# A product-key expert stage on one core: one-hots one step later, index search beside the greatest values, experts' values in six slots

## The reference, cut to what matters

```
xn = batchnorm(x1) * gamma + beta
q = xn @ w_q.T                                  # 2 sides x 8 heads x 128
sim = einsum('pbnhd,hkpd->pbnhk', q, keys)      # 2 sides x 8 heads x 32 keys
s, i = top_k(sim, 8)                            # per side
all_scores = sx[:, None] + sy[None, :]          # 64 sums per token and head
scores, pk = top_k(all_scores, 8)
idx = (ix * 32 + iy)[pk]                        # 8 of 1024 experts
o = gelu(x1 . key_in[idx]) * softmax(scores)
out = layernorm(x1 + sum over head, k of o * key_out[idx])
```

## Time and profile before

| what | value |
|---|---|
| runs of the kernel before | 503.2, 506.0 and 501.16 us; median 503.2 |
| the profiled execution | 506.19 us, with a span of 504.1 us |
| granted clock of TensorE, mean | 0.786 of full speed |
| busy: TensorE, VectorE, ScalarE, GpSimd | 366.8, 431.7, 243.5, 232.1 us |
| scatter, 8192 products of 64x16 | 94.0 us busy |
| experts_out, 1024 products | 90.2 us busy |
| experts_in, 512 products | 68.3 us busy |
| index search, 512 times two instructions | 82.7 and 37.4 us |
| hotx, 32 instructions | 74.9 us |
| weighing on GpSimd, 60 pieces | 77.7 us |

### The profile page before, as it was taken

How to read it: one execution, slowest core, us unless ns; L and a number is a source line. 1 busy time by engine, 2 the same in 40 slices (tenths; PEclk the granted TensorE clock), 3 DMA queues, 4 the chain that set the end, 5 groups by cost and what they waited for, 6 DMA issues and landing times.

```text
span 504.1 us, 24229 instructions
## 1 busy us (share of the span) xinstructions
PE 366.8 (73%) x10097; PEld 268.3 (53%) x10097; DVE 431.7 (86%) x2755; ACT 243.5 (48%) x398; POOL 232.1 (46%) x311
## 2 busy tenths in 40 slices
PE   5979855166647778786888689768787678878755
PEld 3445543034443557465748474646477347746655
DVE  1557986999999689989999999899999997995923
ACT  2897564355324433574365337443754472445222
POOL 1023350542449344646556474647382925282610
PEclk9979956678656877889797678877987796579769
DMA  8900000000000000000000000000000000000001
GB/s 241 180 1 1 1 1 0 1 1 5 3 5 2 3 4 3 5 3 25 6 1 4 25 5 1 6 25 3 3 6 25 3 3 4 25 3 4 23 5 44
DMA packets 7661, 8.95 MB, mean 18 GB/s; under 512 B 896, under 2 KB 6912, under 8 KB 7424
## 3 DMA queue, kind: packets, MB, share of 16 engines
q1 hardware_dynamic: 6976, 7.34, 5.5%
q10 hardware_dynamic: 576, 0.07, 0.1%
HBM read 5.31 MB, written 2.10 MB: 15 GB/s over the span
## 4 chain that ended last, share of the span: by engine, by line
PE 47%; DVE 17%; issue 14%; POOL 5%; ACT 4%; ACTq 0%; DVEq 0%; POOLq 0%
PE psum L895 17%; PE psum L871 13%; PE psum L882 9%; PE psum L851 6%; DVE idx L623 3%; DVE vals L615 3%; DVE picked L648 2%; DVE arena L679 2%; POOL code L259 2%; POOL arena L286 2%; DVE arena L683 1%; DVE arena L682 1%; DVE arena L676 1%; ACT L434 1%; POOL ixf L254 1%
## 5 line engine op out<-in xcount | busy, mean ns | idle before, releaser
L871 PE MATMUL psum<-arena 64*64 64x16 f16 x8192 | 94.0, 180 | 77.5 <-issue 67.1
L871 PEld LDWEIGHTS psum<-arena 64*64 64x64 f16 x8192 | 86.2, 117 | 94.5 <-issue 85.5
L895 PE MATMUL psum<-ko,arena 64*128 64x128 f32 x1024 | 90.2, 353 | 2.0 <-issue 2.0
L895 PEld LDWEIGHTS psum<-ko,arena 64*128 64x128 f32 x1024 | 86.7, 264 | 2.9 <-issue 2.5
L623 DVE FIND_INDEX8 idx<-vals,sims 128x8 uint32<-128x32 f32 x512 | 82.7, 186 | 0.0
L286 POOL TENSOR_TENSOR arena<-arena 128x512 f32<-128x512 f32 x60 | 77.7, 1328 | 4.3 <-ACT arena L426 4.3
L882 PE MATMUL psum<-x1T,trn 128*64 128x256 f32 x512 | 68.3, 423 | 12.6 <-ACT arena L434 12.6
L679 DVE TENSOR_TENSOR arena<-iota,listsT 128x4096 f16<-128x4096 f16 x32 | 74.9, 2339 | 0.0
L426 ACT ACTIVATE arena<-psum 128x1024 f32<-128x1024 f32 x32 | 32.6, 1018 | 72.5 <-PE psum L871 72.5
L882 PEld LDWEIGHTS psum<-x1T,trn 128*64 128x64 f32 x512 | 36.6, 152 | 51.1 <-ACT arena L434 24.3
L239 POOL TENSOR_TENSOR cand<-vals 128x128 f32<-128x128 f32 x16 | 9.4, 588 | 118.0 <-DVE vals L615 118.0
(11 more groups left out here) (117 smaller groups left out, 563.7 us busy)
## 6 DMA issues: line engine op xcount, KB each, us to landing
x<-in_L_attn_x_dram SPq DMA_DIRECT2D x8, 256.0 KB, 4.8
out_dram<-nat SPq DMA_DIRECT2D x7, 256.0 KB, 2.1
ko<-in_L_ffn_key_out_dram SPq DMA_DIRECT2D x2, 512.0 KB, 9.7
nat<-in_L_ffn_key_in_dram SPq DMA_DIRECT2D x2, 256.0 KB, 9.7
nat<-in_L_ffn_keys_dram SPq DMA_DIRECT2D x2, 128.0 KB, 5.6
out_dram<-nat SPq DMA_DIRECT2D x2, 128.0 KB, 1.7
nat<-in_L_attn_W_delta_dram SPq DMA_DIRECT2D x1, 64.0 KB, 2.8
nat<-in_L_attn_W_in_dram SPq DMA_DIRECT2D x1, 64.0 KB, 2.8
```

What stands on the lines that cost most here:

```text
L871: end = pe.matmul(psum[64 * e:64 * e + 64, at:at + NJ], hotx[rows, g, :, e], hotw[rows, part, g, :, e], start=(part == 0), stop=(part == 1))
L895: end = pe.matmul(y2[:, e, m % 2] if m < NS - 1 else y_last[:, e], gl[rows, m % 4, j, :], ko[rows, j, :], start=(j == 0), stop=(j == NJ - 1))
```

## The change

It does these things:

- One-hots, lists, halves and scatter of a step are done one step later than before: VectorE's step m now holds hots_of(m-2), and the loops run to NS + 2. On TensorE the scatter isn't split any more.
- VectorE does indices(m) and top_sums(m) straight after greatest(m), and pack to weights of m-1 after them.
- `weigh` works by halves of the tokens, two pieces each: the second half of step m-4 before the candidate sums, the first of m-3 after them.
- experts_in and gelus run in steps 0, 1, 3, 5 ... 13 in place of 1, 3 ... 15, and `gl` has six slots.
- The two products of hoty with the weight halves become one instruction; listsT is laid out by halves of the tokens for it.
- The scatter halves (14, 1) and (15, 1) go to banks 0 and 1 in place of 2 and 3.

The diff, cut to its core:

```diff
+    GL = 6
+    GELU_STEP = (0,) + tuple(range(1, NS - 2, 2))
...
+        def p_base(m, hf):
+            return 0 if m * 2 + hf in (2 * NS - 3, 2 * NS - 1) else b_p
...
-            def weigh(m):
-                wait(pool, "p_evac", m * 2 + 2)
+            def weigh(m, hf):
+                wait(pool, "p_evac", m * 2 + hf + 1)
                 wait(pool, "gelu_done", (m // 2 + 1) * JR)
...
-            for m in range(NS + 1):
+            for m in range(NS + 2):
+                if m >= 2:
+                    halves(m - 2)
+                if m >= 4:
+                    weigh(m - 4, 1)
                 if m < NS:
                     candidate_sums(m)
-                if m >= 1:
-                    halves(m - 1)
                 if m >= 3:
-                    weigh(m - 3)
+                    weigh(m - 3, 0)
                 if m < NS:
                     candidate_codes(m)
                     over_eighth(m)
...
             def gelus(q):
-                wait(act, "y2_mm", q * 2 - 2)
+                wait(act, "y2_mm", q * 2 - 4)
                 for r in range(JR):
                     if r == 2:
-                        signs(2 * q + 1)
+                        signs(GELU_STEP[q])
...
+            for m in range(NS + 2):
+                if m >= 3:
+                    p_out(m - 3, 0)
                 if m >= 2:
-                    p_out(m - 2, 0)
+                    lists_out(m - 2)
                 if m < NS:
                     exps(m)
...
                 if m + 1 < NS:
                     sims_out(m + 1)
                 if m + 2 < NS:
                     normed(m + 2)
+                if 1 <= m <= NS:
+                    high_copied(m - 1)
+                if m >= 3:
+                    p_out(m - 3, 1)
+                if m < NS:
+                    low_halves(m)
+                if 1 <= m <= NS:
+                    convert(m - 1)
+                if m in GELU_STEP:
+                    gelus(GELU_STEP.index(m))
...
             def indices(m):
+                wait(dve, "code_done", m)
...
             def top_sums(m):
+                wait(dve, "dt_done", m)
...
-                dve.tensor_tensor(hotw[:, 0, at], hoty[:, at], spread(2, NJ), ALU.mult)
-                dve.tensor_tensor(hotw[:, 1, at], hoty[:, at], spread(3, NJ), ALU.mult).then_inc(s["hot_done"], 1)
+                both = listsT[:, hf, 2:4, :].rearrange("p w (g s) -> p (w g) s", s=2).unsqueeze(2)
+                dve.tensor_tensor(hotw[:, :, at].rearrange("p w g j s -> p w (g j s)"),
+                                  hoty[:, at].rearrange("p g j s -> p (g j s)").unsqueeze(1).to_broadcast(
+                                      [P, 2, 32 * NJ * 2]),
+                                  both.to_broadcast([P, 64, NJ, 2]), ALU.mult).then_inc(s["hot_done"], 1)
...
-            for m in range(NS + 1):
+            for m in range(NS + 2):
                 if m < NS:
                     greatest(m)
-                if m >= 1:
+                    indices(m)
+                    top_sums(m)
+                if 1 <= m <= NS:
                     pack(m - 1)
                     pick(m - 1)
                     weights_and_codes(m - 1)
-                if m < NS:
-                    indices(m)
-                    top_sums(m)
-                if m >= 1:
-                    hots_of(m - 1, 0)
-                    if m >= 5 and m % 2:
+                if m >= 2:
+                    hots_of(m - 2, 0)
+                    if 5 <= m < NS and m % 2:
                         residual(m // 2 - 2)
-                    if m >= 6 and m % 2 == 0:
+                    if 6 <= m <= NS and m % 2 == 0:
                         scales(m // 2 - 3)
-                    hots_of(m - 1, 1)
+                    hots_of(m - 2, 1)
...
+            for m in range(NS + 2):
                 if m >= 2:
-                    scatter(m - 2, 1, 0, 12)
-                if 1 <= m < NS:
-                    lists_turned(m - 1)
-                if m >= 2:
-                    scatter(m - 2, 1, 12, 32)
+                    lists_turned(m - 2)
                 if m + 1 < NS:
                     scores(m + 1)
...
+                if m >= 3:
+                    scatter(m - 3, 1)
+                if m >= 4:
+                    wait(pe, "lists_evac", m - 1)
+                    experts_out(m - 4)
+                if m in GELU_STEP:
+                    experts_in(GELU_STEP.index(m))
+                if m >= 2:
+                    scatter(m - 2, 0)
```

## The result

| kernel | runs | median, us | lowest to highest |
|---|---|---|---|
| before | 4 | 504.5 | 501.2 to 506.0 |
| after | 4 | 510.4 | 510.2 to 512.3 |

The measured ratio is 1.017, 95% interval 1.012 to 1.023 (the two medians alone give 1.012): slower, where the forecast was 496 us. That the change is slower is clear of noise; whether it is slower by 2% is not. The profiled execution has a span of 508.4 us; its granted clock is 0.768 (0.786 before).

What follows compares the result with a forecast made beforehand. TensorE bounds, VectorE nearly full. Step 6 at 205 plus five pairs (238) gives 443; the end adds 51.6 and lag up to 2: span 497, plus 2.1 around it, less 3.0 for a slow profiled run: 496 us, range 488 to 508.

Steps and rivals of the forecast that it cites:

- Both own pairs: Each engine's own work in two steps of the expert stage: TensorE 47.6 us, VectorE 46.2 less 0.3 without GpSimd's interference.
- the port's price: VectorE's one-hots lengthened by GpSimd pieces let in between them, through exclusive SBUF access: 1.6 us a pair taken.
- Fill: Pipeline start with one-hots two steps behind: first scatter near 130 us, step 6 at 205, VectorE 9 us ahead.
- words and lists: VectorE's waits for ScalarE's copied words, 9.4 us, and turned lists, 8.3, would go, except 2.6 in step 2.
- The residual's new wait: VectorE's residual needs an experts_out of the same step: zero wait unless TensorE is 3 us late.
- the pair's 3.2: Full cost of GpSimd pieces in VectorE's one-hots, per two steps: 2.3 us in an even step, 0.9 in an odd.
- the alternating kind: Steps where GpSimd gets in between VectorE's one-hots, six before the change; bound 2.3 us even, 0.9 odd.
- seven held steps: Steps before the change where GpSimd waited through VectorE's one-hots at no cost to VectorE; taken as about as frequent.
- 51.6: Time from step 16 to the end, in us, summed from TensorE's scatter halves, experts_out and lists; 48.27 before.
- Held throughout: Rival: GpSimd always waits out the one-hots, VectorE pays nothing, TensorE alone bounds: 491 us, chance 0.17.
- the slow rival: Two later weighing pieces, delayed by TensorE's lag, also fall into the one-hots: 512 us, chance 0.15.
- The full price: Rival: every GpSimd meeting is paid, VectorE's pair 49.1 bounds, step 16 at 453.5: 504 us, chance 0.25.

Runs made afterwards that it cites:

- e10: The kernel before with TensorE's scatter halves cut and interleaved with other products, nothing of the change: 494.3 us, ratio 0.980 to before.
- e1: The kernel after, with GpSimd's halves and two earlier weighing pieces waiting until the previous step's one-hots are done: 502.8 us, ratio 0.996 to before.
- e7: The kernel after with GpSimd waiting for one-hots, high_copied ahead of sims_out, and no scatter products of the weight's second half: 475.9 us, one run.
- e9: The kernel after with TensorE's scatter halves cut and interleaved with other products, no GpSimd waits or moved copy: 511.9 us, ratio 1.013 to before.
- e6: The kernel after with GpSimd waiting for one-hots, high_copied ahead of sims_out, and scatter halves cut and interleaved: 490.9 us, ratio 0.967 to before.
- e4: The kernel after with the one-hots' merged product split into two instructions again: 517.5 us, ratio 1.028 to before.

## Why the prediction was wrong

**The views of before: right.** That both engines are nearly full and TensorE bounds was right: e10 speeds up the kernel before by TensorE's order alone. Both own pairs were right: 47.6 forecast and 47.7 found for TensorE with the port's price gone (e1); 45.9 for VectorE without it (46.2 less 0.3), found in e7.

**Fill, merge, words and lists: right in time.** The first scatter starts at 130.06 (forecast 130.5), step 4 at 158.2 (158); the words' wait in step 2 is 3.2 us (2.6), and all other waits for words and for lists are gone up to the last step. The residual's new wait is 0.9 us, once. The merged product is 1.21 in the second half of a step, as forecast, and 1.45 in the first, where it meets a short GpSimd operation.

**The step that failed: "I take half of the pair's 3.2, 1.6, for both kinds are about as frequent".** The offset had been worked out rightly (0.22 us into the first one-hot), and so had the bound from the alternating kind, 2.3 in an even step and 0.9 in an odd one. The counts of before did not bear on it: all seven held steps had asked within 0.08 us of the first one-hot, and after the change halves() asks 0.21 to 0.22 us into it, every time. (Within 0.08 us is not enough to be held, though: in even steps of the kernel after the second piece asks 0.02 us or less behind the second one-hot's start, and is let in at the next boundary, the 3.35 at 227.02. What separates the two kinds stays open.) The runs show the alternating kind in every step, 2.3 and 0.7 us, 3.0 a pair. VectorE's pair is 48.9, not 47.5, and passes TensorE's 47.7. Step 6 comes 2.0 us late and the ten steps behind it take 6.4 more: 8.4 of the span. With the price of the steps taken in full, the rival's start of step 16, 453.5, was 2 us too late.

**The end was mis-sized: "51.6", with 2 of lag; it took 56.95.** The step behind it is "I take 5.2 us for a half ... and hold that the gap belongs to its 512 instructions, whatever stands around them". TensorE in the last stretch of the kernel after:

```profile
464.05 2.32 PE L888 MATMUL psum<-arena 64*64 64x16 f16 x252
468.86 0.23 PE L888 MATMUL psum<-arena 64*64 64x16 f16 x4 [2.49 <-issue]
469.10 0.38 PE L873 MATMUL psum<-ident,lists 128*128 128x128 f16 x4
469.41 1.45 PE L888 MATMUL psum<-arena 64*64 64x16 f16 x118
472.63 1.89 PE L888 MATMUL psum<-arena 64*64 64x16 f16 x128 [1.77 <-issue]
476.65 0.33 PE L888 MATMUL psum<-arena 64*64 64x16 f16 x10 [2.13 <-issue]
476.91 5.40 PE L911 MATMUL psum<-ko,arena 64*128 64x128 f32 x64
482.24 1.69 PE L888 MATMUL psum<-arena 64*64 64x16 f16 x181
486.31 1.58 PE L888 MATMUL psum<-arena 64*64 64x16 f16 x128 [2.38 <-issue]
489.62 1.89 PE L888 MATMUL psum<-arena 64*64 64x16 f16 x128 [1.72 <-issue]
493.36 1.24 PE L888 MATMUL psum<-arena 64*64 64x16 f16 x75 [1.86 <-issue]
```

scatter(14, 0) starts 12.6 us after step 16, as the sum with its lag had it (12.7). But two halves behind each other, the first with the lists behind it, take 12.9 us for the 10.8 of the sum (464.05 to 476.91), and the next two 12.3 for 10.5 (482.24 to 494.5). A half alone is 5.2 us with one gap; two together have three gaps and at most 1.9 us of work between them. That is 3.9 us; the other terms give 0.5 back, and the end is 3.4 longer than forecast. The granted clock was lower here too, 0.71 for 0.82 before; no run separates what that cost, but one gap more in each of the two places (1.7 to 2.5 us each) is as large as the excess.

**Rivals.** Held throughout: the steps deny it. The late pieces of the slow rival did not come, as TensorE had time to spare. The full price was the right mechanism, forecast at 504 us, a span of 505; the measured span is 508.4, 2 us less up to step 16 and 5.4 more behind it. The other 3 us to 510.4 lie in the last line of the sum: it took 3.0 off because the profiled run of before was slower than its median, and added 2.1 around the span, where the run of after is 2.0 above its span at 510.4 and no slower than its median. So the forecast of 496 missed by 8.4 in the steps, 3.4 in the end and 2.9 there, less 0.3 of rounding. What makes the change slower and not equal is thus the one term in which no rival differed: the end, 8.7 us longer than before, outweighs the 4.4 us that are left of the fill's gain. The sign of my range was carried by the steps, and I had given the end one value only.

## What to carry to other kernels

Where the trace shows two outcomes of the same meeting, don't weigh them by how often each occurs: a new order can put every meeting on one side, as here. Compare each meeting of the changed order with the kinds seen, and if what separates them isn't known, forecast the two ends and not their mean. Give a pipeline that becomes one step deeper its full price at the end, and read that price from a stretch with the same neighbours: a unit's time inside other work (5.2 us) isn't its time behind its like. And when two engines are within 3% of each other, an experiment that relieves one shows only the distance to the next: by the ratios, e1 alone is 2.1% below the kernel after and e9 0.5%, both together (e6, with the copy moved too) 5.0%.

## What the runs showed of the hardware

In the kernel after, a GpSimd instruction that waited for VectorE's one-hots got in at the next boundary between them, and cost VectorE about the same whatever it was let in before: a piece of 128x512 in f32 cost 1.07 us against a one-hot of 2.28 us and 0.87 against an operation on 128x4 of 0.16 us. So the cost goes by how many GpSimd instructions find such a boundary, not by the length of VectorE's. One boundary more (e4) cost 0.8 us in an odd step, where it let in a piece that otherwise passed beside the residual, and nearly nothing in an even one. It is not so always: in the kernel before, GpSimd was held through four or eight instructions in seven steps, at no cost to VectorE, and in eleven steps of e10, each time asking within 0.08 us of the first one-hot; what decides is not shown.

TensorE's issue gaps of 1 us and more stand one block of 256 instructions, or several, apart, and each ends 2.15 to 2.70 us after a 16 KB transfer of instructions starts; 128 short products, with their loads such a block, are 1.24 to 1.9 us of work. Slower products between the runs of 128 brought the gaps before the scatter from 71 to 39 us. The Trainium skill, page "Runtime: NRT & Kernel Launch", section "Instruction fetch mechanics", says that instructions are refilled in blocks of 256, and that the crossing is "mostly hidden". The transfers agree with the block (79 packets of 16 KB, 32 fewer for 8192 instructions fewer); that the crossing is hidden the trace denies where the products are this short.
